# Attention with a feed-forward layer on one core: operand copies issued in parts, and the two late score units of a head moved to places 9 and 13

## What is computed

```python
x = x + attn(layernorm(x))          # 32 query heads (4 groups of 8), 8 key/value heads, head size 16
    # q = x Wq^T; k = x Wk^T; v = x Wv^T
    # probs = softmax(q k^T / 4) over all 2048 keys; a_dot = probs v
    # sigma = elu(q);  a_mem = (sigma memory) / (sigma memory_norm)
    # out = a_dot (1 - w) + a_mem w,  w = sigmoid(memory_weight)
x = x + ffn(layernorm(x))           # input rounded to float8, 512 x 512 weight in float8
```

## Time and profile before

| | us |
|---|---|
| three runs, median (lowest to highest) | 2346.47 (2337.27 to 2348.74) |
| the profiled execution, its own time | 2343.36 |
| its span, first to last instruction | 2341.6 |
| TensorE busy | 1831.6 |
| ScalarE busy | 1898.9 |
| VectorE busy | 1528.0 |
| mean granted clock of TensorE, share of full | 0.923 |

### The profile page before, as it was taken

The page is one execution under the profiler, slowest core; times in us unless marked ns, Lnnn a source line. Parts: engine busy times, 40 slices in busy tenths (PEclk is TensorE's granted clock), DMA queues, the critical chain, the costliest instruction groups (busy, mean ns, idle before and its releaser), DMA issues.

```text
span 2341.6 us, 78599 instructions
## 1 busy us (share of the span) xinstructions
PE 1831.6 (78%) x35892; PEld 678.4 (29%) x35892; DVE 1528.0 (65%) x1746; ACT 1898.9 (81%) x2100; POOL 99.5 (4%) x148
## 2 busy tenths in 40 slices
PE   9996788877777787777777877777787777778776
PEld 7872222222222222222222222222222222222224
DVE  6754777766666667656666766666676567667655
ACT  5556999978887898878788878878888788889787
POOL 5530000000000000000000000000000000000000
PEclk9998999988998999999889889889998999999899
DMA  6551111111102111121111111121101211120111
GB/s 213 202 190 48 44 40 37 33 43 46 46 27 63 46 33 34 45 63 36 37 46 52 32 45 45 28 63 46 41 27 44 63 37 35 46 63 24 42 48 39
DMA packets 131497, 128.34 MB, mean 55 GB/s; under 512 B 30518, under 2 KB 106726, under 8 KB 131174
## 3 DMA queue, kind: packets, MB, share of 16 engines
q1 hardware_dynamic: 130166, 121.55, 18.6%
q10 hardware_dynamic: 1008, 1.84, 0.2%
HBM read 87.36 MB, written 32.24 MB: 51 GB/s over the span
## 4 chain that ended last, share of the span: by engine, by line
PE 27%; ACT 22%; SPq 19%; DVE 18%; DMA 7%; issue 6%; POOL 0%; ACTq 0%; DVEq 0%; POOLq 0%
ACT pool L824 22%; PE ps L1104 12%; DMA q_st<-guard 7%; PE ps L988 7%; SPq L589 5%; PE ps L903 5%; DVE late L1528 4%; SPq L505 3%; SPq L506 3%; SPq L507 2%; SPq L509 2%; DVE late L1536 2%; DVE late L1547 2%; DVE late L1549 2%; DVE v_tiles L1542 2%
## 5 line engine op out<-in xcount | busy, mean ns | idle before, releaser
L824 ACT ACTIVATE pool<-ps 128x1024 f32<-128x1024 f32 x1892 | 1774.2, 1119 | 346.1 <-PE ps L988 341.7
L988 PE MATMUL ps<-q_st,k_st 51*32 51x512 f16 x16128 | 803.5, 408 | 480.6 <-DMA q_st<-guard 233.5
L1104 PE MATMUL ps<-pool,v_st 64*32 64x512 f32 x16128 | 1127.0, 627 | 6.1 <-DVE by_token L1558 6.1
L988 PEld LDWEIGHTS ps<-q_st,k_st 51*32 51x32 f16 x16128 | 232.1, 94 | 1396.6 <-ACT pool L824 749.5
L1528 DVE TENSOR_SCALAR late<-ps 128x1024 f32<-128x1024 f32 x124 | 146.1, 1219 | 417.6 <-PE ps L988 417.6
L1104 PEld LDWEIGHTS ps<-pool,v_st 64*32 64x32 f32 x16128 | 300.0, 111 | 144.4 <-issue 73.8
L1558 DVE STREAM_TRANSPOSE by_token<-ps 128x512 f32<-128x512 f32 x126 | 82.7, 694 | 173.8 <-PE ps L1104 173.8
L1552 DVE SCALAR_TENSOR_TENSOR pool<-late 128x2048 f32<-128x2048 f32 x62 | 142.1, 2292 | 11.2 <-PE ps L1104 9.1
L1536 DVE SCALAR_TENSOR_TENSOR late<-late 128x2048 f32<-128x2048 f32 x62 | 142.1, 2293 | 2.1
L1549 DVE SCALAR_TENSOR_TENSOR late<-late,v_tiles 128x2048 f32<-128x2048 f32 x62 | 142.1, 2292 | 2.1
L1547 DVE SCALAR_TENSOR_TENSOR late<-v_tiles 128x2048 f32<-128x2048 f32 x62 | 141.8, 2287 | 1.2
(11 more groups left out here) (169 smaller groups left out, 1030.1 us busy)
## 6 DMA issues: line engine op xcount, KB each, us to landing
q_st<-q_aug SPq DMA_DIRECT2D x128, 128.0 KB
k_st<-k_aug SPq DMA_DIRECT2D x128, 128.0 KB
v_st<-v_aug SPq DMA_DIRECT2D x64, 256.0 KB
sigma_kept<-y_out SPq DMA_DIRECT2D x32, 256.0 KB, 2.0
q_aug<-parts SPq DMA_DIRECT2D x32, 256.0 KB, 2.7
q_st<-q_aug SPq DMA_DIRECT2D x128, 64.0 KB
k_st<-k_aug SPq DMA_DIRECT2D x128, 64.0 KB
wqT<-sigma_kept SPq DMA_DIRECT2D x32, 256.0 KB, 3.0
```

Of the source, the lines that this page charges most:

```text
L824: act.activation(held[:, half_u * 2 * CH:half_u * 2 * CH + 2 * CH], sc[slot_of("exp", unit)].rearrange("p a b -> p (a b)"), ACT.Exp, scale ...
L988: last = pe.matmul(dst[VW * c:VW * c + VW, x, :], k_st[RT * x:RT * x + AUG, par, keys:keys + VW], q_st[RT * x:RT * x + AUG, par, q * CH:q ...
L1104: last = pe.matmul(acc[r][VW * c:VW * c + VW, :].rearrange("v (i s) -> v i s", s=VW), v_st[rows, par, j, :], by_place[rows, c, :, :], star ...
```

## The change

- The semaphore operands_loaded of a parity counts the ten copies of q, k and guard; v has its own, values_loaded, which TensorE waits for before a head's first weighing.
- load_block waits for scores_ready, that all 30 exp units of head n - 2 are scored, before q, k and guard, and for pv_done, as before, only ahead of v. The guard goes ahead of v.
- turn_tile moves from behind load_block of an odd head into load_block of the next even head, between the guard and the wait for pv_done. store_chunk(g - 2) moves from ahead of load_block(g, 2) to behind it.
- The machine loop over chunks 2 to 7 becomes a Python loop: the instructions are written out.
- LATE_AT becomes (9, 13); the order of slots follows from it.
- TensorE's wait at the head's start stays only in heads whose late units nobody scored ahead.

```diff
-HEAD_LOADS = QK_LOADS + ROW_TILES + 1
+SCORE_LOADS = QK_LOADS + ROW_TILES
-LATE_AT = (11, 12)
+LATE_AT = (9, 13)
+        values_loaded = [sem(f"values_loaded{i}") for i in range(2)]
             def load_v(g, h, par):
                 sp.dma_start(v_st[:, par, :, :].rearrange("p (c t) w -> p c (t w)", c=CPB), v_src((g // CPB) * CPB, h))\
-                    .then_inc(operands_loaded[par], 16)
+                    .then_inc(values_loaded[par], 16)
-            def load_block(g, h):
+            def load_block(g, h, tile=None):
                 n = g * HEADS + h
                 par = h % 2
+                sp.wait_ge(scores_ready, 2 * LATE_TILE * (n - 1) + 2)
+                load_qk(n, g, h, par, operands_loaded[par])
+                load_guard(g, h, par, operands_loaded[par])
+                if tile is not None:
+                    turn_tile(tile)
                 sp.wait_ge(pv_done, (n - 1) * ST)
-                load_qk(n, g, h, par, operands_loaded[par])
                 load_v(g, h, par)
-                load_guard(g, h, par, operands_loaded[par])
                 if par == 0:
                     load_sigma(g * QG + h // 2)
-            for h in range(2, HEADS):
-                load_block(0, h)
+            for h in range(2, HEADS):
+                load_block(0, h)
             for h in range(HEADS):
-                load_block(1, h)
-                if h % 2 == 1:
-                    turn_tile(h // 2)
-            with sp.Fori(2, NG) as g:
+                load_block(1, h, h // 2 - 1 if h % 2 == 0 and h > 0 else None)
+            for g in range(2, NG):
                 for h in range(HEADS):
+                    load_block(g, h, (g - 1) * TPC + h // 2 - 1 if h % 2 == 0 else None)
                     if h == 2:
                         store_chunk(g - 2)
-                    load_block(g, h)
-                    if h % 2 == 1:
-                        turn_tile((g - 1) * TPC + h // 2)
+            turn_tile((NG - 1) * TPC - 1)
             store_chunk(NG - 2)
             def late_scored(n, x):
                 if x == 0:
-                    pe.wait_ge(operands_loaded[n % 2], (n // 2 + 1) * 16 * HEAD_LOADS)
+                    pe.wait_ge(operands_loaded[n % 2], (n // 2 + 1) * 16 * SCORE_LOADS)
             def weigh_v(n, j):
                 if j == 0:
+                    pe.wait_ge(values_loaded[n % 2], n // 2 * 16 + 16)
             def head(n):
                 par, pair = n % 2, n // 2
-                pe.wait_ge(operands_loaded[par], (pair + 1) * 16 * HEAD_LOADS)
+                if not has_late(n):
+                    pe.wait_ge(operands_loaded[par], (pair + 1) * 16 * SCORE_LOADS)
             for n in range(LAST_HEAD):
                 head(n)
-            pe.wait_ge(operands_loaded[1], (LAST_HEAD // 2 + 1) * 16 * HEAD_LOADS)
+            pe.wait_ge(operands_loaded[1], (LAST_HEAD // 2 + 1) * 16 * SCORE_LOADS)
+            pe.wait_ge(values_loaded[1], LAST_HEAD // 2 * 16 + 16)
```

More of the change, by code:

```diff
@@ L547, in _ @@
                 for par in range(2):
-                    sp.wait_ge(operands_loaded[par], 16 * HEAD_LOADS)
+                    sp.wait_ge(operands_loaded[par], 16 * SCORE_LOADS)
                 with sp.Fori(0, NG) as g:
@@ L1016, in last_chunk @@
                 pe.wait_ge(key_ones_loaded, 16 * ROW_TILES)
-                pe.wait_ge(operands_loaded[0], 16 * HEAD_LOADS)
+                pe.wait_ge(operands_loaded[0], 16 * SCORE_LOADS)
                 score_early(0)
```

## The result

The changed kernel takes 2066.18 us (median of 4 runs, 2065.12 to 2066.85) against 2343.99 for the kernel before in the same session: a ratio of 0.8816 (95% interval 0.8792 to 0.8840), 278 us less.

What follows compares the result with a forecast made beforehand. No engine is full; ScalarE and TensorE wait for operand copies held in SyncE's queue. Savings of 255 us over 26 pairs, 13 in heads 2 to 8, 8 and 1 at heads 61 and 0 total 277, giving 2066 us, range 2040 to 2140.

Steps and rivals of the forecast that it cites:

- a pair: An odd and an even head together: 55.7 us without gaps plus 0.8 and 1.55, so 58.05 against 67.86.
- Start of the copies: SyncE's q, k and guard copies begin at T - 1.8; operands ready at T + 5.7, within T + 4.6 and T + 8.2.
- T - 1.8: T is a head's first exponential; copies were to begin 1.8 us before it, instead of T + 1.6 (even) or T + 5.4 (odd).
- The stall goes to 0: ScalarE's gap before late units, 4.79 us in the row and 233.5 in all, vanishes with the half clock behind it.
- Even head: Gaps booked for an even head: 0.17 + 0.55 + 0.1 = 0.8 us, with 0.4 at unit 11 and 0.15 at unit 9.
- Odd head: Gaps booked for an odd head: 0.6 at the FFN product, 0.7 at unit 21, 0.1 for a full TensorE; 1.55 us.
- that hides, but for 0.15 on unit 7: VectorE's sums 0.9 us late in odd heads, first weighing moved from 3.1 to 4.0 us; only 0.15 us shows.
- a falling clock behind late operands: Rival, 14%: operands land at T + 8.2, TensorE's clock falls; 2139 us, or 2190 if both kinds of head suffer.
- the second rival: TensorE's short pauses at the late units alone keep its clock falling, 1.11 + 0.53 us a head: pair 61.3, 2167 us; 3%.
- the third one: VectorE becomes the bound: second late unit taken 1 us later than counted, 1.5 us more a pair, 2113 us; 14%.
- The loop: SyncE's loop over chunks written out: booked at 0 us, together with the separate semaphore and one wait per head.
- The slots: Late units at 9 and 13: no wait for copies; the 0.53 of two adjacent late units taken as 0 in odd heads.

## Why the prediction was right

The time, 2066.2, is the forecast to the microsecond, and a pair 58.01 against 58.05. The mechanism was right, but that the sum is so exact is luck: an even head came out 0.48 us shorter than counted and the odd heads 0.42 us longer on the mean (29.82 against 29.40), and these two made up for each other. The early heads and the end held: 13 us were counted before head 9 and 12.7 came, 8 behind head 61 and 7.8 came.

- **Start of the copies.** T - 1.8 predicted; they begin at T - 1.8 in odd heads and T - 1.9 in even ones. Ready at T + 5.7 predicted: by the run with the transposes put back, a first late unit is taken 8.26 us after the first issue, 0.5 to 0.7 us of which are its own scoring, so ready at about T + 5.8. Here too two errors met. What I took off for v, 1 us, measured 1.6 to 1.7 with its issue of 0.4, within the bounds; and the 8.5 us that I took it from was the row of head 31, which is the mildest of the 27 odd heads. On the mean of the kernel before scoring starts 9.15 us after the first issue, the stall at unit 11 is 7.0 us and not 4.79, and the copies of odd heads start at T + 7.2 and not at T + 5.4. The forecast did not hang on that stall or that start, since it went by the measured length of a pair. In odd head 23 of the run with the transposes put back (from 923.0) the guard's last issue ends at 936.0, and the first late unit is taken 16.1 us into the head, at 939.1, of which 0.7 is its scoring; the copies were there some 2.4 us after that issue. The Trainium skill (DMA: Bandwidth & Descriptors, Anatomy of one DMA) gives about 2.0 us fixed, setup and completion together, for a software-issued DMA. The profile lists SyncE's copies as hardware_dynamic, so they are of another kind; the trace comes near that figure, at 2.4.
- **The stall goes to 0.** Right: none of the 233.5 us is left. Its cause was as said: putting the transposes back costs 258 us, the old wait 69. The slack was larger than counted: TensorE comes to the first late unit of an odd head at T + 7.4 or later, not at T + 6.7.
- **Even head.** 0.8 us of gaps predicted, 0.30 found (0.17 at unit 7, 0.13 at unit 11), and a head of 28.17 us instead of 28.65. I mis-sized the first late unit's wait for VectorE, booked at 0.55 with its echo at unit 9: VectorE takes the slot at T + 8.95, as counted, but unit 11 needs only 0.13 us more. The 0.1 for a full TensorE does not show.
- **Odd head.** 0.6 and 0.7 predicted at units 19 and 21, 0.46 and 0.60 found; my own two times for unit 21, 20.7 and 20.1, give 0.6, not 0.7. VectorE's lateness was right (sums at 2.6 predicted, 2.8 found), but the step "that hides, but for 0.15 on unit 7" failed: TensorE's idling drops its clock in 12 of 27 odd heads, 1.69 us each, 0.75 a pair. I had priced a falling clock behind late operands and behind short pauses at the late units, each in a rival, and neither here. It is of the second rival's kind, with a quarter of its price (0.75 us a pair against 3.3), set off by what the third one feared, VectorE being late for the sums.
- **The loop.** "0" was wrong for the kernel before, where it is worth 0.8%. In the changed kernel SyncE waits 1222.1 us for scores, so there it should be hidden; this was not tried, as no run keeps the loop with the new wait.
- **The slots.** Right that 9 and 13 need operands early, and that the later second unit costs. Wrong to book the 0.53 behind the late units of the kernel before as the price of adjacency: at 11 and 12 with early operands it is 0. The change as a whole is worth 278 us; everything in it but the late places is worth 331 (2347.68 against 2017.02 in the same session).

## What to carry to other kernels

Read what stands ahead of a late transfer in its queue before shortening the transfer: here an instruction that waited for another engine held up copies that had nothing to do with it. When one limit is lifted, look again at parts of the change that were made for it, and try each alone; here one of them cost 49 us. In a chain that hands over between engines, a wait of about 1 us that buffers hide can still show through a lower clock; here 1.1 us did and 0.5 us did not. And before working from the rows of one head, look how it stands among the others: the one used here was the mildest of 27, and only other errors made up for it.

## What the runs showed of the hardware

TensorE's granted clock fell from 2.4 to 1.2 GHz (0.57 of full over 4 us, between its two levels) behind two pauses of 0.51 and 0.75 us with one score unit of 0.41 between them, in 12 of 27 odd heads, 1.69 us each. In the other 15, with the same pauses (0.51 and 0.74 in head 31), it stayed at 2.4 GHz. With the second pause at 0.13 us (places 11 and 12) or gone (the shorter VectorE chain) the granted clock is 1.00 over 52 heads.

Behind the guard's last issue the operand copies were there after 2.5 us on the mean where v does not stand ahead of the guard (2.3 to 3.1, transposes put back, copies for even heads), as far as the start of TensorE's scoring shows it.

Writing out a loop on the DMA-issuing engine shortened the issue of eleven copies from 6.4 to 6.1 us on the mean and gave 0.8% on the whole, though SyncE spends most of its time waiting. Which of the loop's branches and the address arithmetic costs this was not separated.
